# A gated transformer on one core: the matmuls of constants between a pair's transposes and its logits are taken out of two expert stages

## The reference

```python
def _L0_ffn_ref(tokens, router_w, router_b, expert_weights):          # 8 experts, one matrix each
    logits = jnp.einsum('bsh,eh->bse', tokens, router_w) + router_b
    probs = jax.nn.softmax(logits, axis=-1)
    top_p, top_i = jax.lax.top_k(probs, TOP_K)                        # TOP_K = 2
    w = top_p / (jnp.sum(top_p, axis=-1, keepdims=True) + EPS)
    ...
    y_all = jnp.einsum('nh,ehd->ned', x, expert_weights)
    y_k = jnp.take_along_axis(y_all, idx[:, :, None], axis=1)
    out = jnp.einsum('nk,nkh->nh', wf, y_k)
    ...
def _L1_ffn_ref(x, Wr, W1, b1, W2, b2):                               # 8 experts of 512 hidden, 20 slots each
    capacity = int(T / E * CAP_FACTOR)
    probs = jax.nn.softmax(x @ Wr, axis=-1)
    topk_probs, topk_experts = jax.lax.top_k(probs, K)
    ...
    h = jax.nn.relu(jnp.einsum('ebnc,ech->ebnh', buf, W1) + b1[:, None, None, :])
    y = jnp.einsum('ebnh,ehc->ebnc', h, W2) + b2[:, None, None, :]
    ...
```

## Time and profile before

| | |
|---|---|
| median of 3 runs | 1738.1 us (1736.13 to 1740.51) |
| the profiled execution | 1735.85 us |
| its span, first to last instruction | 1734.1 us |
| mean granted TensorE clock over the span | 0.96 |
| busy: TensorE, its weight loads, VectorE, ScalarE, GpSimd | 91%, 61%, 61%, 54%, 33% of the span |
| linear experts, from its first matmul of constants to its first expert matmul | 210.0 to 241.65 us |
| capacity experts, from its first matmul of constants to its count of tokens | 760.5 to 787.6 us |

### The profile page before, as it was taken

How to read it: one execution, slowest core, us unless ns; L and a number is a source line. 1 busy time by engine, 2 the same in 40 slices (tenths; PEclk the granted TensorE clock), 3 DMA queues, 4 the chain that set the end, 5 groups by cost and what they waited for, 6 DMA issues and landing times. The chain is left out here.

```text
span 1734.1 us, 46162 instructions
## 1 busy us (share of the span) xinstructions
PE 1575.9 (91%) x17384; PEld 1055.1 (61%) x17384; DVE 1065.2 (61%) x2300; ACT 933.3 (54%) x2341; POOL 570.1 (33%) x1033
## 2 busy tenths in 40 slices
PE   3998799999999999988987799979999987998898
PEld 1555454677777777765775456646777754555354
DVE  5687777666666666644166788962322235877676
ACT  3787535555655555544444566534443336875354
POOL 4565328133232332311122344300000004664772
PEclk8999899999999999989999899979999997999899
DMA  8444230000000000010104434110000016541000
GB/s 191 136 134 127 72 79 0 10 8 8 5 8 4 8 8 5 2 50 13 37 1 99 109 104 113 31 38 0 1 0 0 0 46 148 152 140 56 7 19 25
DMA packets 114002, 86.41 MB, mean 50 GB/s; under 512 B 19344, under 2 KB 110736, under 8 KB 113808
## 3 DMA queue, kind: packets, MB, share of 16 engines
q1 hardware_dynamic: 106592, 81.30, 17.1%
q10 hardware_dynamic: 7216, 2.45, 0.9%
HBM read 22.88 MB, written 2.10 MB: 14 GB/s over the span
## 5 line engine op out<-in xcount | busy, mean ns | idle before, releaser
L1105 DVE TENSOR_REDUCE neg_max<-scores 128x8 f32<-128x1024 f32 x192 | 226.7, 1181 | 73.0 <-PE scores L723 28.4
L2205 POOL TENSOR_TENSOR probs<-probs,inverse 128x512 f32<-128x512 f32 x128 | 133.1, 1040 | 314.6 <-DVE inverse L2410 314.4
L2344 ACT ACTIVATE probs<-scores,neg_max 128x128 f32<-128x128 f32 x512 | 180.7, 387 | 5.3 <-DVE neg_max L2402 5.3
L969 ACT ACTIVATE probs<-turned 128x1024 bf16<-128x1024 f32 (+1 forms) x128 | 131.1, 1024 | 85.1 <-PE turned L746 85.0
L1863 ACT ACTIVATE hidden_f<-hb_f,b_f 128x512 f32<-128x512 f32 x128 | 88.0, 687 | 128.8 <-PE hb_f L1809 128.5
L554 POOL TENSOR_TENSOR k_all<-k_all,k_parts 128x512 f32<-128x512 f32 x24 | 27.8, 1158 | 322.3 <-ACT k_parts L895 322.3
L1818 PEld LDWEIGHTS yb_f<-w_f,hidden_f 128*128 128x128 f32 x1024 | 119.2, 192 | 14.8 <-issue 14.8
L2335 ACT ACTIVATE heads_t<-heads 128x512 f32<-128x512 f32 x64 | 38.2, 597 | 166.4 <-PE heads L2270 166.4
L1818 PE MATMUL yb_f<-w_f,hidden_f 128*128 128x128 f32 x1024 | 119.3, 275 | 0.0
L1809 PE MATMUL hb_f<-xn_all_f,w_f 128*128 (+1 forms) x256 | 116.8, 600 | 0.0
L2344 ACT ACTIVATION_READ_ACCUMULATOR probs<-scores,neg_max 128x1 f32 x512 | 116.7, 228 | 0.0
(11 more groups left out here) (348 smaller groups left out, 3766.9 us busy)
## 6 DMA issues: line engine op xcount, KB each, us to landing
k_rep<-k_parts SPq DMA_DIRECT2D x144, 128.0 KB, 2.6
q_rep<-q_parts SPq DMA_DIRECT2D x129, 128.0 KB, 2.5
dense<-both SPq DMA_DIRECT2D x120, 64.0 KB, 2.1
ctx_t<-in_ctx_t_dram SPq DMA_DIRECT2D x24, 256.0 KB, 3.7
conv_weights_or_copies<-k_parts SPq DMA_DIRECT2D x32, 128.0 KB, 2.6
conv_weights_or_copies<-q_parts SPq DMA_DIRECT2D x32, 128.0 KB, 2.5
w_f<-in_L_ffn_W_dram SPq DMA_DIRECT2D x16, 256.0 KB, 3.4
x_state<-in_x_dram SPq DMA_DIRECT2D x4, 512.0 KB, 7.9
```

Source lines behind the costliest of these rows:

```text
L969: nc.scalar.activation(probs[:, b % 2, pair, :], turned[:, :], ACT.Exp, **bias).then_inc(s["exp_done"], 1)
L1105: v.tensor_reduce(neg_max[:, b % 2, 8 * pair + first:8 * pair + 8], scores[pair][:, first * S:].rearrange("p (h k) -> p h k", k=S), axis=X ...
L2205: nc.gpsimd.tensor_tensor(p4, p4, inverse[:, n % 2, CH * h:CH * h + CH].unsqueeze(2).to_broadcast([P, CH, S]), ALU.mult).then_inc(s["prob_ ...
L2344: last = nc.scalar.activation(probs[:, n % 2, h, c * S:(c + 1) * S], scores[n % 2][:, i * S:(i + 1) * S], ACT.Exp, bias=neg_max[:, n % 2, ...
```

## The change

One line goes from the feed loop of each of the two stages: the single matmul of constants in every turn. Each loop has 16 turns, so 32 matmuls go. The runs of constants ahead of the feeds and behind them stay.

```diff
@@ -1347,7 +1347,6 @@
             for p in range(NP):
                 if p + 1 < NP:
                     feed.tensor(pe, p + 1, (p + 1) % 2, 0)
-                keep_clock(nc, st, bank[7][:, :], 1)
                 logits_of(p)
 
             def experts(p, r):
@@ -1505,7 +1504,6 @@
             pe.wait_ge(st.loads["capacity"].sem, st.loads["capacity"].total)
 
             def logits_of(p, r):
-                keep_clock(nc, st, bank[0][:, :], 1)
                 pe.wait_ge(feed.xnt_done, p + 1)
                 for u in range(2):
                     last = nc.tensor.matmul(logits[:, bass.ds(p * 2 * E + u * E, E)], feed.xn_t[:, r, u * S:(u + 1) * S],
```

## The result

| | before | changed |
|---|---|---|
| median | 1738.88 us (19 runs, 1733.02 to 1746.72) | 1745.66 us (19 runs, 1740.20 to 1753.02) |
| ratio | | 1.0038, 95% interval 1.0026 to 1.0051 |
| span of the profiled execution | 1734.1 us | 1744.5 us |
| mean granted clock | 0.96 | 0.95 |

What follows compares the result with a forecast made beforehand. TensorE was taken to set both feed loops. Feed losses and clock regained behind them, 3.8 + 4.2 - 0.85 - 0.25 = +6.9 us, moved the median from 1738.1 to 1745.0 us, range 1736.0 to 1749.5.

Steps and rivals of the forecast that it cites:

- Steps 1 and 2: Both feeds: a keep costs 0.22 us; logits waiting on ScalarE's copy (the ring) limit full-clock steps to 0.72 and 0.68 us.
- a keep lies fully on the path: Both feed loops: TensorE, busy without a break, sets the steps of 0.82 and 0.81 us, so each keep adds its time.
- Step 3: Both feeds: without the 512-column matmuls, transposes and short logits matmuls do not hold the clock, which falls to 0.50.
- Step 4: Both feeds: at half clock (1.2 GHz), six f32 weight loads of 0.195 us or more make a step 1.25 us.
- The rival of unslowed loads: Both feeds: clock falls but a weight load stays at 0.11 us, total 1737.1 us; chance 0.10.
- Step 5: Feeds: steps at full, then half clock; middle of early and late falls gives linear experts +3.8 us, capacity experts +4.2.
- the forecast's early end: Feeds: the clock holds some 3.4 us after its rise; linear experts +4.6 us, capacity experts +5.2.
- the late case: Feeds: opening keeps make the clock hold as long again; linear experts +2.1 us, capacity experts +2.3.
- Step 6: Behind the feeds: smaller idle gap, experts may begin at full clock, -0.85 us; matmul that counts tokens -0.25 us.
- sign that the six other stages are as long as before: Outside the two edited stages: unchanged stage lengths, listed among the signs that would show the prediction right.
- The one in which the ring binds: Both feeds: clock stays up and the wait for ScalarE's copy sets the step; -3.5 us, 1734.6 us; chance 0.08.
- The other, with turns of 0.60 us: Both feeds: clock stays up and TensorE still sets the step; -6.6 us, 1731.5 us; chance 0.05.

Runs made afterwards that it cites:

- e6: Kernel before, with two 512-column matmuls of constants instead of one in every turn of both feeds; 1739.69 us (one run).
- e1: Kernel before, with the matmul of constants deleted only from the feed of linear experts; 1743.46 us, ratio 1.0025.
- e2: Kernel before, with the matmul of constants deleted only from the feed of capacity experts; 1741.36 us, ratio 1.0020.
- e7: Kernel before, with the matmul of constants in both feeds replaced by an f32 one of 8 columns; 1750.7 us, ratio 1.0080.
- e11: Changed kernel, with 36 instead of 44 and 16 instead of 24 matmuls of constants behind the feeds; 1752.99 us (two runs), ratio to kernel before 1.0072.
- e8: Kernel before, with 63 instead of 44 and 44 instead of 24 matmuls of constants behind the feeds; 1737.81 us, ratio 0.9994.
- e3: Kernel before, with 256 instead of 512 columns in the matmul of constants in every turn of both feeds; 1740.68 us, ratio 1.0005.
- e9: Kernel before, with 256 columns in every turn of both feeds and the longer runs of constants behind them (63 and 44); 1735.29 us, ratio 0.9967.
- e5: Kernel before, with the 512-column matmul of constants only in every second turn of both feeds; 1739.32 us, ratio 1.0011.
- e4: Kernel before, with 128 instead of 512 columns in the matmul of constants in every turn of both feeds; 1741.63 us, ratio 1.0010.

## Why the prediction was right

It said 1745.0 us and the median is 1745.66; +6.9 was forecast, +6.8 measured. The steps:

- Steps 1 and 2 (keep and ring): right, though the sentence above them that a keep lies fully on the path is so only for a second keep (e6). At full clock the changed turn averages (221.00 - 218.10) / 4 = 0.72 us over four turns of the matmuls of logits, 0.72 was forecast; 256 columns give 0.73. The idle time before every second load of logits is laid to ScalarE's copy (0.20 above), so the ring is what binds there.
- Step 3 (the clock falls in both feeds): right, and shown for each feed alone by e1 and e2. That busy time does not hold it was argued from the logits of the gelu stage and is shown by e7.
- Step 4 (a turn at half clock): 1.17 us, 1.25 forecast. Six loads at the 0.195 that the earlier trace rows gave make 1.17; I had rounded up towards 0.21, and should not have. The rival of unslowed loads (0.85 a turn) is out. The Trainium skill, "TensorE: Matmul & The Clock Gate", section "LDWEIGHTS (loading the stationary operand)", divides the columns by 1.2 GHz whatever the clock, an estimate of 0.11 us for 128 columns; the trace agrees at 1.00 (six loads in 0.61) and not at 0.50.
- Step 5 (how long the clock holds): the mechanism is right, the sizes offset each other. The middle of early and late was taken. Counted from its rise, the clock of the changed kernel held for the early 3.4 us in both feeds. But it rose later than in the trace of before, 0.4 us behind the first logits and 0.9 ahead of them, where the sum had 1.0 and 1.7 ahead from the earlier trace rows. So it fell 3.9 and 2.5 us behind the first logits, between the forecast's early end (2.4 and 1.6) and its late one (5.8 and 5.0). The early end with 1.17 a turn would have been about +4.1 and +4.6 by the sum's own way; F and the surplus of R give +3.2 and +3.5, for +3.8 and +4.2 forecast. e2 and e11 show the late case (F +1.4 to +1.9). Which of the two an execution gets, the prediction could not know.
- Step 6 (what comes back): -0.85 was half of 1.7, since the experts "may" begin at full clock. In the profile of the changed kernel they did, and 1.5 us came back; in e1, with the same linear experts and the same small gap, the clock fell and nothing came back. So one half is a fair term for a gap of this size. Behind the count -0.25 was forecast. Nothing came back in the changed kernel (+0.1), where the clock fell directly behind the count, and 0.6 in e2, where it did not. That a gap fully closed keeps the clock is shown by e8.
- Not in the forecast: the opening of each stage took 0.35 us more (O), in an execution in which the clock rose later after the opening keeps. O also varies without any edit before it (4.4 to 5.5 in the table), so it is not put down to the change. The prediction's sign that the six other stages are as long as before holds only within some 2 us, and they move that much without this edit too.

The match to 0.1 us of the size is luck in part: the terms of the two feeds came out 0.6 and 0.7 us under their forecast and step 6 gave 0.3 us more back, while the openings added 0.7 us that no term had. So the stages hold 6.0 us by the profile, and the medians could lie 2.2 us off either way by their interval.

The opposite rivals, both with a clock that stays up, are refuted for this edit. The one in which the ring binds is what e3 and e9 show with 256 columns kept in each turn: full clock and 0.73 us a turn. The other, with turns of 0.60 us, was seen nowhere.

Left open: what decides when the clock falls in a gap of 1.8 to 3.0 us, and why a stretch at half clock behind a gap lasts 3.4 us in some profiles and 6.8 in others. The second goes with the moment of the fall. In the six cases of 6.8 us (both stages of e3 and e5, capacity experts of e4 and e11) the clock fell 1.0 to 2.2 us before TensorE's next matmul; in the eleven cases of 3.4 us it fell at most 0.5 us before it or up to 0.9 behind it. What sets that moment, no run here shows.

## What to carry to other kernels

A matmul whose result nobody reads can be worth more than its time: look at the granted clock before and behind it, not at its place on the critical path, and price its removal by the work that follows at half clock. Ask how little of it is enough (here 256 columns a turn instead of 512) and where else the same loop runs without it (here the gelu feed). And close the idle gap behind a shortened part fully, in the same edit. With the gap closed the clock stayed up in six cases of six, with a small one in three of seven; with the gap open, e3 lost there what its feeds had gained.

## What the runs showed that I had not expected

With 128 columns a turn, the clock held through one feed and fell after 10.2 us in the other, in the same execution. One and the same stage, linear experts of the changed kernel and of e1, kept its clock behind the feed in one profile and lost it in the other. A load of f32 weights with next to nothing behind it follows the matmul clock: six in 0.61 to 0.62 us in the unhindered turns at 1.00 and in 1.17 us at 0.50; the eight of e7 took 0.84 and 1.60.
